# Six of sixteen state outputs of a selective scan are added up by accumulating DMAs in HBM instead of by TensorE

## The reference, cut to what matters

```python
def step(state, xs):
    d_t, B_t, C_t, u_t = xs
    dA = jnp.exp(d_t[..., None] * A)                        # (b, e, n)
    state = state * dA + (d_t * u_t)[..., None] * B_t[:, None, :]
    y_t = jnp.einsum('ben,bn->be', state, C_t)              # the sum over the 16 states
    return (state, y_t)
y = y + D[None, :, None] * u
y = y * silu(z)                                             # z is the layer norm of x
x = x + tanh(g) * y
```

## Time and profile before

| | |
|---|---|
| median of 3 runs | 4009.07 us (4008.64 to 4009.97) |
| profiled execution | 4009.79 us, of it span 4008.2 us |
| mean granted TensorE clock | 0.968 of full speed |
| PE busy | 3712.5 us (93%) |
| DVE busy | 2989.2 us (75%) |
| ACT busy | 1753.3 us (44%) |
| POOL busy | 644.6 us (16%) |
| line 1193, sums by identity | 512 records, 241.4 us |

### The profile page before, as it was taken

The page is one execution under the profiler, slowest core; times in us unless marked ns, Lnnn a source line. Parts: engine busy times, 40 slices in busy tenths (PEclk is TensorE's granted clock), DMA queues, the critical chain, the costliest instruction groups (busy, mean ns, idle before and its releaser), DMA issues.

```text
span 4008.2 us, 40981 instructions
## 1 busy us (share of the span) xinstructions
PE 3712.5 (93%) x12733; PEld 1926.3 (48%) x12786; DVE 2989.2 (75%) x4855; ACT 1753.3 (44%) x2732; POOL 644.6 (16%) x595
## 2 busy tenths in 40 slices
PE   7888888899999998899999999899999999999787
PEld 4555555544444444444447444455455455454343
DVE  5788788888979788888898655477277277377498
ACT  5767676733323322444343111155155255254276
POOL 2233232234434110343411000000000000000000
PEclk9999999999999999999999999999999999999899
DMA  4232232433233322444425000121011021012000
GB/s 138 75 108 85 97 106 71 155 119 139 99 139 112 129 76 86 148 163 141 147 96 212 31 32 21 66 74 56 29 65 61 24 74 52 32 65 75 0 11 32
DMA packets 91724, 344.89 MB, mean 86 GB/s; under 512 B 11776, under 2 KB 20096, under 8 KB 78112
## 3 DMA queue, kind: packets, MB, share of 16 engines
q1 hardware_dynamic: 63040, 230.05, 16.1%
q0 software_dynamic: 28512, 112.74, 8.3%
HBM read 280.36 MB, written 62.39 MB: 86 GB/s over the span
## 4 chain that ended last, share of the span: by engine, by line
PE 55%; DVE 25%; issue 11%; ACT 6%; DMA 2%; DVEq 0%; ACTq 0%; POOL 0%; SPq 0%; POOLq 0%
PE ps L1115 36%; PE ps L1498 5%; PE ps L1193 3%; PE ps L1488 3%; PE ps L1375 3%; DVE room L1646 2%; PE ps L1324 2%; DVE room L1650 2%; DVE room L1654 2%; ACT room L802 1%; DMA room<-bc_scratch 1%; DVE room L1659 1%; DVE stat L1610 1%; PE ps L1183 1%; DVE stat L2147 1%
## 5 line engine op out<-in xcount | busy, mean ns | idle before, releaser
L1115 PE MATMUL ps<-lnT,room 128*128 128x512 f32 x2240 | 993.5, 599 | 28.0 <-DVE room L1855 12.6
L1115 PE MATMUL ps<-room 128*128 128x512 bf16 (+2 forms) x3001 | 960.7, 477 | 58.2 <-DVE xres L2131 20.7
L1115 PEld LDWEIGHTS ps<-lnT,room 128*128 128x128 f32 x2240 | 427.8, 192 | 578.2 <-issue 535.8
L1115 PEld LDWEIGHTS ps<-room 128*128 128x128 bf16 (+1 forms) x3040 | 420.7, 141 | 575.7 <-issue 320.5
L632 POOL TENSOR_TENSOR idle<-idle 128x1 f32<-128x1 f32 x268 | 469.0, 1750 | 1324.9 <-ACT room L812 508.5
L1324 PE MATMUL ps<-room 128*128 128x512 f32 x864 | 377.9, 595 | 7.3 <-DVE room L1806 7.3
L739 ACT ACTIVATE room<-room,small 128x511 f32<-128x511 f32 x256 | 163.6, 710 | 365.7 <-DVE room L1650 365.6
L1703 DVE TENSOR_TENSOR_SCAN room<-room 128x2048 f32<-128x2048 f32 x64 | 283.1, 4424 | 10.9 <-ACT room L802 4.8
L1650 DVE TENSOR_TENSOR_SCAN room<-room 128x2048 f32<-128x2048 f32 x64 | 283.3, 4427 | 5.4
L2095 DVE TENSOR_REDUCE stat<-ps 128x1 f32<-128x512 f32 x256 | 177.0, 691 | 132.3 <-PE ps L1115 132.3
L1324 PEld LDWEIGHTS ps<-room 128*128 128x128 f32 x864 | 164.2, 191 | 213.2 <-issue 207.4
(11 more groups left out here) (222 smaller groups left out, 4889.5 us busy)
## 6 DMA issues: line engine op xcount, KB each, us to landing
room<-in_ffn SPq DMA_DIRECT2D x16, 2048.0 KB, 10.6
room<-bc_scratch POOLq DMA_DIRECT2D x128, 256.0 KB, 3.6
room<-kv_stash SPq DMA_DIRECT2D x64, 512.0 KB, 3.3
kv_stash<-room POOLq DMA_DIRECT2D x96, 256.0 KB, 2.3
room<-stash POOLq DMA_DIRECT2D x24, 1024.0 KB, 5.2
room<-in_ffn SPq DMA_DIRECT2D x20, 1024.0 KB, 5.5
room<-in_ffn SPq DMA_DIRECT2D x12, 1536.0 KB, 8.4
room<-in_head SPq DMA_DIRECT2D x68, 256.0 KB, 3.8
```

Source lines behind the costliest of these rows:

```text
L1115: last = nc.tensor.matmul(out, lhsT, rhs, start=(i == 0), stop=(i == len(parts) - 1))
```

## The change

Within a batch, the states 1, 3, 5, 7, 9 and 11 (`ACC`) are no longer summed by PE. ACT writes their turned, C-scaled copy to another buffer, `m_acc` (the place of the last batch's x in SBUF, and in the last batch the free `m_nd`), and POOL sends it as a DMA of 1 MB to a tensor `acc_stash` in HBM: a plain store for state 1, an accumulating one (`accum_op=ALU.add`) for the other five. At n = 13 SP loads the result back (1 MB, into `m_acc`), and PE adds it at n = 14 as if it were one state. PE so does eleven sums in a batch instead of sixteen.

New waits: ACT, before it writes an odd state from 3 on, waits for the landing of the DMA of the odd state before; POOL does the same before it issues; SP at n = 13 waits for the landing of all six, ahead of the three `stash` stores and of the row of state 14; PE at n = 14 waits for the load. The x of the last batch is loaded by SP at the start of the last batch instead of at the start of the kernel, and the stage-1 weights wait until PE has summed the loaded array in the last batch.

```diff
+ACC = (1, 3, 5, 7, 9, 11)
+ACC_LOAD, ACC_AT = 13, 14
+ACC_SUMMED = sum(n not in ACC for n in range(ACC_AT)) + 1
+SUMS = DS - len(ACC) + 1
...
+        acc_stash = nc.dram_tensor("acc_stash", (P, NE * S), F32, kind="Internal").ap()
...
+        m_acc = (xres[:, (B - 1) * NT * D:B * NT * D], m_nd)
...
# SP
+                    if last:
+                        sp.wait_ge(nsum_done, (B - 2) * SUMS + ACC_SUMMED)
+                        load_x(B - 1)
                     for n in range(DS):
...
+                        if n == ACC_LOAD:
+                            sp.wait_ge(acc_added, b * (len(ACC) * 16) + len(ACC) * 16)
+                            sp.dma_start(m_acc[last], acc_stash).then_inc(acc_loaded, 16)
                         if n == 13:
                             places = [stashed(a, b) for a in range(3)]
                             sp.wait_ge(stash_ready, b + 1)
...
                 sp.wait_ge(stash_stored, B * 48)
+                sp.wait_ge(nsum_done, (B - 1) * SUMS + ACC_SUMMED)
...
# POOL
+                count = b * KV_WAITS + KV_FIRST
+                for n in range(DS):
+                    if n in ACC:
+                        if n > ACC[0]:
+                            pool.wait_ge(acc_added, b * (len(ACC) * 16) + ACC.index(n) * 16)
+                        wait(tile_taken, tile("h", n, NT - 1)[0] + 1, count)
+                        count += 1
+                        pool.dma_start(acc_stash, m_acc[last] if n % 2 else m_hT, accum_op=ALU.add if n > ACC[0] else ALU.bypass
+                                       ).then_inc(acc_added, 16)
+                    i = kv_slot(n, last)
...
# ACT
+                        turned = t3(m_acc[last] if n in ACC and n % 2 else m_hT, NT)
+                        sent = sum(m in ACC for m in range(n - 1))
+                        if n - 2 in ACC and (n in ACC or n % 2 == 0):
+                            act.wait_ge(acc_added, b * (len(ACC) * 16) + sent * 16)
...
-                            nc.scalar.activation(hT3[:, t, :], ps[:, bank, :], ACT.Copy,
+                            nc.scalar.activation(turned[:, t, :], ps[:, bank, :], ACT.Copy,
...
# PE
-                        for t in range(NT):
-                            pe.wait_ge(tile_taken, tile("h", n, t)[0] + 1)
-                            mm = nc.tensor.matmul(ps[:, t, :], ident[:, :], hT3[:, t, :], start=(n == 0), stop=(n == DS - 1))
-                        mm.then_inc(nsum_done, 1)
+                        if n == ACC_AT:
+                            pe.wait_ge(acc_loaded, b * 16 + 16)
+                            for t in range(NT):
+                                mm = nc.tensor.matmul(ps[:, t, :], ident[:, :], t3(m_acc[last], NT)[:, t, :], start=False, stop=False)
+                            mm.then_inc(nsum_done, 1)
+                        if n not in ACC:
+                            for t in range(NT):
+                                pe.wait_ge(tile_taken, tile("h", n, t)[0] + 1)
+                                mm = nc.tensor.matmul(ps[:, t, :], ident[:, :], hT3[:, t, :], start=(n == 0), stop=(n == DS - 1))
+                            mm.then_inc(nsum_done, 1)
...
# DVE
+                            if last:
+                                dve.wait_ge(x_loaded, 16 * B)
                             layernorm(stage, b)
...
-                    dve.wait_ge(nsum_done, b * DS + DS)
+                    dve.wait_ge(nsum_done, b * SUMS + SUMS)
```

More of the change, by code:

```diff
@@ L278, in flamingo @@
             sem("delta_ready"), sem("dA_ready"), sem("scan_done"), sem("nsum_done"))
+        acc_added, acc_loaded = sem("acc_added"), sem("acc_loaded")
         y_ready = sem("y_ready")
@@ L429, in _, with load_x @@
                 sp.dma_start(m_kvw[h], head_d[h * P:(h + 1) * P, HEAD_Q:]).then_inc(kvw_first, 16)
-            for b in range(B):
+            def load_x(b):
                 sp.dma_start(t3(xres[:, b * NT * D:(b + 1) * NT * D], NT),
                              x_d[b * S:(b + 1) * S, :].rearrange("(t p) d -> p t d", p=P)).then_inc(x_loaded, 16)
+            for b in range(B - 1):
+                load_x(b)
             def load_ctx(b, used, value):
@@ L632, in wait @@
                 nc.gpsimd.tensor_tensor(idle[:, :], idle[:, :], idle[:, :], ALU.add).then_inc(zeros_added, 1)
-            KV_FIRST, KV_WAITS = 2 * KV_LEAD, 2 * KV_HEADS
+            KV_FIRST, KV_WAITS = 2 * KV_LEAD, 2 * KV_HEADS + len(ACC)
             KV_ALL = KV_WAITS * B
@@ L649, in store_kv @@
                 slots = KV_HEADS - KV_LEAD if last else KV_HEADS
[L650 to L655, removed]
+                count = b * KV_WAITS + KV_FIRST
[8 more added lines that the diff above has]
+                    i = kv_slot(n, last)
+                    if i is not None:
+                        h = (KV_LEAD + i) % KV_HEADS
+                        place = kv_stashed(b + (1 if i >= KV_HEADS - KV_LEAD else 0), h)
+                        store_unit(place, [tile("kv", i, half)[0] for half in range(2)], count,
+                                   None if last and i + 2 >= slots else (h + 2) % KV_HEADS, i)
+                        count += 2
             def store_late(k):
@@ L1765, in mamba @@
                 state_of(0, 0)
-                dve.wait_ge(x_loaded, 16 * B)
+                dve.wait_ge(x_loaded, 16 * (B - 1))
                 front = 3 + 1
```

## The result

The changed kernel takes 4099.4 us (median of 4 runs, 4096.3 to 4104.7), the kernel before, on the same chip, 4009.5 (4008.6 to 4012.6). The ratio is 1.0224, with a 95% interval of 1.0206 to 1.0242: 90 us slower. The profiled execution of after took 4096.95 us, of it span 4095.1. The forecast was 4059, the range 4008 to 4130; the forecast's own range, without its rivals, was 4040 to 4085.

The account below looks back on a forecast made before the run. PE, DVE and ACT were read as close together, none full, with PE and ACT handing the batch to each other. 35 us in three looped batches plus 15 in the last made 50, so 4059 us; range 4008 to 4130.

Parts of the forecast that it names:

- rival A: The accumulating DMA is slow, over 12 us, so head stores behind it stall ACT: 4110 to 4155 us; chance 0.22.
- The sums that go: Six PE sums a batch removed: 2.1 us gained per looped batch, from states 3 and 5; the others about nothing.
- The sum that comes: PE's added sum at state 14, between transposes and sum, where PE has no gap: full price, 3.4 us a batch.
- X: Time of the 1 MB accumulating DMA from POOL: between 5.3 and 10.5 us, taken as 8.
- When the last DMA goes out: Third batch: h(11) copied by 598.6, 2.1 us gained; its DMA sent at 600.9, landed at 608.9.
- From that landing to DVE's state 14: SP's queue: row of 14 lands 12.7 us after the landing, plus 3 for the load ahead, at 624.7.
- From state 14 to PE's product: DVE's scan, `take_next`, ACT's decay and copies: from 624.7 to PE's product at 637.1, 8.3 us late.
- The last batch: Softplus 5.6 us earlier, h(11) copied at 770.6, state 14 11.6 late; 15.0 with the added sum.
- Edits at nothing: ACT's and POOL's DMA waits, head stores, last batch's x and stage-1 weights: no cost, weights at most 3 us.
- B: SP's wait is hidden, the accumulate takes about 5 us, the row isn't held up: +2, 4011 us; chance 0.12.
- C: PE bounds the stage, so all net sums count: 69 us faster, 3940 us; chance 0.08.
- The signs: Expected profile: x352 sums, accumulate near 8 us, DVE waiting 12 to 14 at state 14, PE busy down about 17.

Follow-up runs that it names:

- run 8: The kernel before without the six sums of states 1, 3, 5, 7, 9 and 11, nothing in their place: 4006.3 us, 0.9991.
- run 9: The kernel before without the six sums, but with one added sum on PE at state 14, without DMAs: 4020.7 us, 1.0031.
- run 4: The changed kernel with six plain stores in place of one plain and five accumulating ones: 4069.5 us, 1.0152.
- Run 6: The changed kernel with SP issuing the row of state 11 ahead of its wait for a head's product and the context load: 4096.0 us, 1.0218.
- run 5: The changed kernel with state 9 summed by PE as before, so five DMAs (1, 3, 5, 7, 11): 4086.3 us, 1.0197.
- run 1: The changed kernel with SP's wait for the six DMAs and the load of their sum moved behind the row of state 15: 4042.2 us, 1.0089.
- run 2: The changed kernel with the three stash stores issued ahead of SP's wait; load and row of 14 stay behind it: 4063.9 us, 1.0138.
- run 3: The changed kernel with state 11 summed by PE as before, so five DMAs (1, 3, 5, 7, 9): 4037.5 us, 1.0069.
- run 10: The kernel before plus the six DMAs with ACT's and POOL's waits; PE sums all sixteen, nothing loaded back: 4026.0 us, 1.0048.
- run 7: The kernel before with the row of state 11 ahead of the head's-product wait and context load in SP's queue: 4010.9 us, 1.0001.
- run 12: The kernel before without the six sums, with one filler product on PE before the head's product of state 8: 4005.0 us, 0.9984.

## Why the prediction was right, and where it was short

The sign, the place and the mechanism were right. The size was short by 40 us, nearly all of it in two terms. The stated range of 4008 to 4130 holds 4099 because it was widened for rival A, a slow accumulate, which didn't come; the forecast's own 4040 to 4085 doesn't hold it.

- **The sums that go.** 2.1 us a looped batch and 5.6 in the last were forecast for states 3 and 5. In after the copy of h(6) is 2.2 earlier and the last batch's softplus 5.6. But run 8 shows that even this isn't kept: a looped batch without any of the six sums takes as long as with them. The step I left out is that products get slower when sums go: in run 8 that of state 8, after 5.8 us of idling instead of 2.4, takes 5.8 to 6.3 us instead of 3.7, and that of state 6 5.1 to 6.2 instead of 5.4. I had put 1.7 a batch for it into the range, not the sum. I also misread the six waits of rows 3: they stand ahead of the products of states 6, 7, 8, 9, 11 and 13, so PE waited behind the sum of state 7 but not behind those of 9 and 11. Run 8 gives these two sums no worth either.
- **The sum that comes.** 3.4 forecast, 3.43 in the timeline, 3.6 by run 9.
- **X.** 8 forecast, 7.8 measured for state 11. The Trainium skill ("Collectives: The Full Stack", "The bandwidth ceiling: the fold count and why AG ≠ RS ≠ AR"; "DMA: Bandwidth & Descriptors", "Anatomy of one DMA — SWDGE (gpsimd) path") gave an estimate of 6.8; the trace has 7.7 against 4.2 plain, so adding costs 3.5 where the half rate gives 2.4 (an estimate from these pages, 1 MB more at 436e3 bytes per us): the measured one decides. X itself wasn't missed. What was: its adding counts twice in a looped batch (run 4).
- **When the last DMA goes out: the first mis-sized term.** I let h(11) be copied 2.1 us early. It was 6.3 late (645.24 - 40.64 = 604.6 against 598.26, rows 5), 8.4 off. I had walked the states to 6 and not from there to 11. Run 6 splits the 8.4: some 3 are row 11, late beside the accumulate of state 9 (the runs 4 and 5 move that wait as theory says), and 5.4 are PE and ACT, with the products of states 8 and 10 at 6.6 and 5.9 us instead of 3.7. Of these 5.4, 3.2 come with the missing sums alone: run 8, without any DMA, copies h(11) 1.1 late and not 2.1 early. Where the other 2.2 come from isn't shown. POOL gave 1.0 back (1.3 from copy to issue, not 2.3), X 0.2.
- **From that landing to DVE's state 14.** 12.7 + 3 = 15.7 forecast, 17.3 measured (656.72 to 674.05). With 8.4 - 1.2 = 7.2 from above and 1.6 from here, DVE is 22.5 late instead of 13.8. Runs 1, 2 and 3 each show that this wait is on the path.
- **From state 14 to PE's product.** 12.4 forecast (624.7 to 637.1), 12.6 measured. With 3.4 of the sum that makes 17.2 + 3.4 = 20.6 a looped batch, of which 20.0 are seen at its end; forecast 11.7.
- **The last batch: the second mis-sized term.** 15 forecast, 25 measured. The copy of h(11) ends at 839.5, that is 778.9 on the clock of before (60.61 earlier), not 770.6: 8.3 late. DVE's state 11 comes 1.7 us early instead of 5.6, because ACT waits 7.7 us for the head's store of state 7: the accumulate of state 7, sent ahead of that store, took 10.2 us to land, and the store behind it 9.7. I had put this edit at nothing. The rest of the 8.3 is PE, whose next product took 6.41 us after 5.67 of idling, where it took 3.69. With plain stores (run 4) ACT's wait is 3.6 and DVE's state 11 isn't held up.

```profile
811.94 1.24 ACT L845 ACTIVATE room<-ps 128x512 f32<-128x512 f32 x2 [7.73 <-DMA kv_stash<-room]
```

So state 14 is 18.9 late, not 11.6, and then PE, at the lower clock after 17.9 us of idling (granted clock 0.50 from 870.7 to 875.0), takes 3.68 for transposes of 1.91 and 4.60 for the first sum instead of 3.60, together 2.8; with the sum, 18.8 + 3.4 + 2.8 = 25.0.

```profile
863.98 2.29 DVE L1744 TENSOR_TENSOR room<-room 128x2048 f32<-128x2048 f32 x1 [18.89 <-DMA room<-bc_scratch]
...
870.78 3.68 PE L1220 MATMUL ps<-ident,room 128*128 128x128 f32 x16 [17.87 <-DVE room L1746]
874.25 4.60 PE L1231 MATMUL ps<-room,ident 128*128 128x512 f32 x8
878.69 3.60 PE L1236 MATMUL ps<-room,ident 128*128 128x512 f32 x8
```

- **Edits at nothing.** The load of x and the weights of stage 1 cost nothing, as said: the first product stands 0.92 us behind ACT in both kernels. POOL's head stores behind the accumulate did cost: ACT waits 11.4 us in all for them, 7.7 of it in the last batch, as told above. I had said that this cover ends at X near 8 to 10, but had taken it from state 11 of a looped batch and given it no price:

```profile
ACT room L845 <- DMA kv_stash<-room: 11.4, 4, 7.7
```

- **Rivals.** A (slow accumulate) is refuted by 7.7 us, though its mark, ACT waiting for `kv_stash`, is there: I had given that mark to A alone. B (SP's wait is hidden) is refuted by run 1. C (PE is the bound) is refuted by run 8: with all six sums gone and none added the kernel gains 2.7 us and stage 0 7.9, not 82 (24 sums of 3.43).
- **The signs.** The accumulate near 8 us and the 352 records came as said. DVE's wait at state 14 was 16.1 to 17.1 and 18.9 us, not 12 to 14, and PE's busy time in the third batch fell by 3.6, not 17: that was the slower products again.

As a check of the whole: no sums -2.7 (run 8), sum at 14 +14.4 (run 9), DMAs +17 (run 10), SP's place +57.2 (run 1). Together 85.9 of 90, if the parts may be added. The remaining 4 us weren't told apart: runs 8 to 10 add up to 28.7, run 1 has 33.2.

What stays open: why the product of 14 takes 3.7 us in one kernel or batch and 5.3 to 6.6 in another after the same 8 + 2 us of idling. The granted clock goes with it (0.82 against 0.55), but no run here sets it at will. Open, too, is why the later stages of run 8 took 6.3 us longer.

## What to carry to other kernels

A wait put into a queue costs by what stands behind it: here a row of 256 KB that DVE needed stood behind the wait, a load and three stores that nobody needed soon, and this made 57 of 90 us; moving the wait, or dropping the last of the six DMAs, gave them back. Before taking work from the engine with the highest busy share, leave the work out altogether and run that: it gave 2.7 us of the 82 that a count of instructions promises. Where a matmul engine is made to wait longer, price the products behind the wait by rows of products that follow a wait; and of a wait seen in a profile ask, as in run 7, what is late next.

## What the runs showed that I had not expected

- An accumulating DMA of 1 MB from SBUF to HBM lands in 7.7 us (median of 18 DMAs, three of them plain), at the most in 10.2, a plain one in 4.2; POOL spends 0.90 us on its issue against 0.55, and a row of 256 KB that goes out beside it takes longer: DVE waits 12.2 us for it, 9.0 beside a plain store and 7.0 beside none.
- A row of 256 KB issued right behind 4 MB of its queue takes 14.7 us to land, right behind a load of 1 MB 7.4 (run 2).
- The same product of 16 matmuls took 3.7, 5.4 or up to 6.8 us in one stage of one kernel. It was longer after longer idling (run 12), but not by the idling alone.
